# Cross attention with a ternary feed-forward on one core: high and low keys of four heads stacked on 64 rows

## The reference, cut to what matters

```
q = layernorm(x) @ Wq + bq          # 32 x 56 x 128, split in 16 heads of 8
k = ctx @ Wk + bk                   # 32 x 1500 x 128
v = ctx @ Wv + bv
scores = einsum('bhqd,bhkd->bhqk', q, k) / sqrt(8)
scores = where(mask == 0, -1e9, scores)
out = softmax(scores) @ v           # heads joined again, 32 x 56 x 128
x = x + out @ Wo + bo
x = x + bitlinear(gelu(bitlinear(layernorm(x), w1)), w2)
```

## Time and profile before

| | us |
|---|---|
| median of 3 runs | 959.67 |
| lowest and highest run | 958.06, 964.99 |
| profiled execution | 959.75 |
| its span | 958.0 |
| TensorE busy | 887.8 (93%) |
| VectorE busy | 753.1 (79%) |
| ScalarE busy | 673.4 (70%) |
| GpSimd busy | 231.5 (24%) |

### The profile page before, as it was taken

How to read it: one execution, slowest core, us unless ns; L and a number is a source line. 1 busy time by engine, 2 the same in 40 slices (tenths; PEclk the granted TensorE clock), 3 DMA queues, 4 the chain that set the end, 5 groups by cost and what they waited for, 6 DMA issues and landing times.

```text
span 958.0 us, 33628 instructions
## 1 busy us (share of the span) xinstructions
PE 887.8 (93%) x11716; PEld 694.2 (72%) x11716; DVE 753.1 (79%) x2593; ACT 673.4 (70%) x1272; POOL 231.5 (24%) x253
## 2 busy tenths in 40 slices
PE   3767989999999999999999999999999999999983
PEld 2344767777787787778787777777787777778772
DVE  3687568888788878888788888888787888888744
ACT  2543667777887877777886777777887777777661
POOL 6310142230222222130222222131222222031200
PEclk9788999999999999999999999999999999999997
DMA  5520221122222211122222211122222111220000
GB/s 130 127 62 1 63 61 29 42 57 60 63 60 63 59 34 47 46 60 60 63 60 63 53 32 50 51 60 60 63 60 61 49 32 50 56 60 0 4 2 6
DMA packets 59375, 49.34 MB, mean 52 GB/s; under 512 B 2785, under 2 KB 55633, under 8 KB 59345
## 3 DMA queue, kind: packets, MB, share of 16 engines
q1 hardware_dynamic: 57551, 48.11, 19.0%
q10 hardware_dynamic: 1793, 0.83, 0.4%
HBM read 47.91 MB, written 0.92 MB: 51 GB/s over the span
## 4 chain that ended last, share of the span: by engine, by line
issue 66%; POOL 18%; PE 7%; DVE 5%; ACT 1%; DMA 1%; POOLq 1%; DVEq 0%; ACTq 0%
POOL k_lo L573 8%; POOL qry_hi L565 4%; POOL qry_lo L566 4%; PE ps_p L820 2%; DMA ctx_sb<-in_ctx_dram 1%; PE ps_p L803 1%; DVE max_junk L1091 1%; POOL q_lo L563 1%; POOL q_hi L562 1%; PE ps_v L856 1%; PE ps_p L744 1%; ACT probs L659 1%; POOL x_rows L581 0%; PE ps_p L741 0%; POOLq L556 0%
## 5 line engine op out<-in xcount | busy, mean ns | idle before, releaser
L1091 DVE CUSTOM_DVE_ANT_0 max_junk<-ps_p,mask_bias 120x500 bf16<-120x500 f32 x768 | 481.6, 675 | 125.3 <-PE ps_p L803 104.5
L659 ACT ACTIVATE probs<-ps_p 125x448 f32<-125x448 f32 x768 | 359.3, 551 | 87.0 <-PE ps_p L820 81.6
L573 POOL TENSOR_TENSOR k_lo<-k_full,k_hi 128x500 fp32r<-128x500 f32 x96 | 119.8, 1262 | 592.0 <-ACT k_hi L651 587.2
L856 PE MATMUL ps_v<-probs,vals 125*32 125x112 f32 x6144 | 162.9, 262 | 0.8 <-issue 0.4
L803 PE MATMUL ps_p<-k_hi,qry_hi 64*120 64x500 f32 x768 | 148.8, 413 | 15.6 <-POOL qry_hi L565 6.5
L820 PE MATMUL ps_p<-qry_hi,k_hi 64*125 64x448 f32 x768 | 158.6, 403 | 4.4 <-DVE seg_max L1091 1.7
L856 PEld LDWEIGHTS ps_v<-probs,vals 125*32 125x32 f32 x6144 | 146.9, 111 | 21.1 <-issue 17.7
L641 ACT ACTIVATE k_full<-ps_p,bk_sb 128x500 f32<-128x500 f32 x96 | 64.7, 674 | 123.1 <-PE ps_p L744 122.6
L820 PE MATMUL ps_p<-own_query,mask_bias 57*125 57x448 f32 x768 | 145.7, 368 | 0.0
L820 PE MATMUL ps_p<-qry_lo,k_hi 64*125 64x448 f32 x768 | 144.4, 366 | 0.0
L820 PE MATMUL ps_p<-qry_hi,k_lo 64*125 64x448 f32 x768 | 144.3, 365 | 0.0
(11 more groups left out here) (124 smaller groups left out, 831.5 us busy)
## 6 DMA issues: line engine op xcount, KB each, us to landing
ctx_sb<-in_ctx_dram SPq DMA_DIRECT2D x31, 750.0 KB
mask_sb<-in_mask_Bx1xSxS_ik_dram SPq DMA_DIRECT2D x64, 328.1 KB
own_query<-shift SPq DMA_DIRECT2D x64, 1.8 KB
out_dram<-x_rows SPq DMA_DIRECT2D x16, 56.0 KB, 1.6
ctx_sb<-in_ctx_dram ACTq DMA_DIRECT2D x1, 750.0 KB
x_rows<-in_x_dram SPq DMA_DIRECT2D x1, 672.0 KB, 10.9
w_sb<-in_L_ffn_w_dram SPq DMA_DIRECT2D x2, 256.0 KB, 8.8
x_rows<-in_x_dram SPq DMA_DIRECT2D x1, 224.0 KB, 5.9
```

The source lines that it names most:

```text
L573: pool.tensor_tensor(k_lo[:, p, at], k_full[:, (p + n) % 2, :], k_hi[:, p, at].bitcast(F32), ALU.subtract)\
L659: act.activation(probs[:, c % NP, h], ps_p[0:KC, BANK[how]["S", c, h], 0:HC], ACT.Exp)\
L856: mm = pe.matmul(ps_v[r:r + VT, col:col + PAIR], vals[:, p, c, t].rearrange("p a r -> p (a r)"), src, start=(c == 0 and t < 4), stop=(c == ...
L1091: dve.tensor_tensor_reduce(max_junk[0:MROWS, BANK[how][slot], :], ps_p[0:MROWS, BANK[how][slot], 0:SEG], mask_bias[0:MROWS, p, s * SEG:(s ...
```

## The change

The keys of a batch now lie in one array `keys` of two planes, 128 rows each. In plane 0 a half of 64 rows holds the high keys of its first four heads (32 rows) and their low keys (32 rows); in plane 1 it holds the low keys of the last four heads and their high keys. ScalarE writes the high part of all rows into both planes with one copy of 2 x 500 elements (`high_keys`). GpSimd makes the low part in a buffer of its own (`k_lo`, two segments deep), and SP moves it by DMA, 32 rows x 500 at a time, over the rows in `keys` that are to hold it (`place_low`, four DMAs a segment, three segments a batch). The queries are projected twice, so that the query of a head stands on both of its sets of rows (`wq_sb` with two planes of columns, `q_all`, `q_flag`, `q_hi`, `q_lo` twice as wide). `qry_lo` is masked with `head_of_high`, which has zeros on the rows of low keys.

A block of scores is now, for each four heads, one product of 64 rows with `qry_hi` (high and low keys at once) and one with `qry_lo`, each of 4 x 56 = 224 columns, and then the product with mask and shift of 448 columns. The maxima multiply the stacked rows too: as many matmuls of 500 columns as before, but they wait for the DMAs of the low keys. The probabilities get eight buffers instead of twelve.

```diff
+GH = HH // 2
+GR = GH * HD
-NP = NC
+NP = 2 * NG
...
-    "T0 T1 T2 X0 Q0 K0 K1 K2 F0",
+    "T0 T1 T2 X0 Q0 Q1 K0 K1 K2 F0",
...
+            def place_low(bt, n):
+
+                b, k, p = bt
+                made = NSEG * b + n + 1
+                at = slice(n * SEG, (n + 1) * SEG)
+                sp.wait_ge(k_lo_ready, made if isinstance(b, int) else sp.snap(made))
+                for h in range(2):
+                    for g in range(2):
+                        src, dst = SLOT * h + GR * g, SLOT * h + GR * (1 - g)
+                        sp.dma_start(keys[dst:dst + GR, p, g, at].bitcast(F32), k_lo[src:src + GR, (p + n) % 2, :].bitcast(F32))\
+                            .then_inc(k_lo_placed[p][n], 16)
...
-                put_q(pool.tensor_tensor(q_hi[:], q_flag[:], ones_f[:, 0:SQ], ALU.mult))
-                put_q(pool.tensor_tensor(q_lo[:], q_flag[:], q_hi[:].bitcast(F32), ALU.subtract))
+                put_q(pool.tensor_tensor(flat(q_hi[:]), flat(q_flag[:]), ones_f[:, 0:2 * SQ], ALU.mult))
+                put_q(pool.tensor_tensor(flat(q_lo[:]), flat(q_flag[:]), flat(q_hi[:].bitcast(F32)), ALU.subtract))
...
                 pool.wait_ge(k_hi_ready, NSEG * b + n + 1)
+                if n == 2:
+                    pool.wait_ge(k_lo_placed[p][0], 64 * (k + 1))
+                else:
+                    wait(pool, k_lo_placed[1 - p][n + 1], 64 * (k + p))
+                pool.tensor_tensor(k_lo[:, (p + n) % 2, :], k_full[:, (p + n) % 2, :],
+                                   keys[:, p, 0, at].bitcast(F32), ALU.subtract)\
...
-                act.activation(k_hi[:, p, at], k_full[:, (p + n) % 2, :], ACT.Copy).then_inc(k_hi_ready, 1)
+                act.activation(keys[:, p, :, at],
+                               k_full[:, (p + n) % 2, :].rearrange("p (g k) -> p g k", g=1).to_broadcast([D, 2, SEG]),
+                               ACT.Copy).then_inc(k_hi_ready, 1)
...
                 if r == 0:
-                    pe.wait_ge(k_hi_ready, NSEG * b + s + 1)
+                    pe.wait_ge(k_lo_placed[p][s], 64 * (k + 1))
...
-                products = [(hi, q_hi_of, HR), (lo, q_hi_of, HR), (hi, q_lo_of, HR),
-                            (bias, own_query[:, p, :, :], SQ + 1)]
-                for n in range(first, last):
-                    key, query, rows = products[n]
-                    for h in range(2):
-                        part = slice(SLOT * h, SLOT * h + rows)
-                        mm = pe.matmul(ps_p[0:KC, BANK[how]["S", c, h], 0:HC].rearrange("k (a q) -> k a q", a=HH),
-                                       key[part, :], query[part], start=(n == 0), stop=(n == 3))
+                for g in range(2):
+                    heads = slice(GH * g, GH * (g + 1))
+                    for part, query in enumerate((qry_hi[:, p, heads, 0:SQ], qry_lo[:, p, heads, :])):
+                        for h in range(2):
+                            rows = slice(SLOT * h, SLOT * (h + 1))
+                            pe.matmul(score_bank(c, h, how)[:, heads, :], keys[rows, p, g, at], query[rows],
+                                      start=(g == 0 and part == 0), stop=False,
+                                      skip_group_check=True)
```

More of the change, by code:

```diff
@@ L144 @@
 DVE_PASS = passes(
-    "Q0 some F0 bias0 bias1 bias2",
+    "Q0 Q1 some F0 bias0 bias1 bias2",
     " ".join(f"m{n}" for n in range(16)) + " some " + " ".join(f"m{n}" for n in range(16, 21))
@@ L262, in xattn_ffn @@
         some_diag = sb("some_diag", [128, SQ], BF16)
-        q_flag = sb("q_flag", [D, SQ])
-        q_hi = sb("q_hi", [D, SQ], F32R)
-        q_lo = sb("q_lo", [D, SQ], F32R)
+        q_flag = sb("q_flag", [D, 2, SQ])
+        q_hi = sb("q_hi", [D, 2, SQ], F32R)
+        q_lo = sb("q_lo", [D, 2, SQ], F32R)
         max_junk = sb("max_junk", [128, NBANK, SEG], BF16)
@@ L307, in xattn_ffn @@
         k_lo_ready = sem("k_lo_ready")
+        k_lo_placed = [[sem(f"k_lo_placed{p}_{n}") for n in range(NSEG)] for p in range(2)]
         vals_ready = sem("vals_ready")
@@ L474, in _ @@
             sp.dma_start(w2_sb[:], w2).then_inc(ff_loaded, 16)
+            for n in range(NSEG):
+                place_low(batch(0, 0), n)
             sp.dma_start(wo_sb[:], wo).then_inc(wo_loaded, 16)
@@ L484, in _ @@
                     sp.dma_start(wo_rows[VT * g:VT * g + VH, t, :], wo[at:at + VH, :]).then_inc(wo_rows_loaded, 16)
+            for n in range(NSEG):
+                place_low(batch(0, 1), n)
             place_shift(batch(0, 0))
@@ L757, in fill @@
                 elif kind == "Q":
-                    mm = pe.matmul(bank[:, 0:4 * PAIR], wq_sb[:], xnt[:, n % 2, :], start=True, stop=True)
+                    mm = pe.matmul(bank[:, 0:4 * PAIR], wq_sb[:, n % 2], xnt[:, n // 2 % 2, :], start=True, stop=True)
                 elif kind == "Z":
```

120 lines of the change are left out of this document (81 added, 39 removed).

## The result

| | before | changed |
|---|---|---|
| median of 4 runs, us | 959.49 | 998.32 |
| lowest and highest run | 958.06, 964.99 | 992.09, 1001.43 |
| span of the profiled execution | 958.0 | 996.6 |
| loop on TensorE, us a turn (pair of batches) | 54.16 | 56.46 |
| first turn ends at | 186.0 | 194.2 |

The ratio is 1.039, with a 95% interval of 1.033 to 1.045: slower, where 934 us had been forecast. A turn is the distance of two taken branches of TensorE's loop, as a mean over 13. The 38.6 us of the spans are 8.2 at the start, 13 x 2.30 = 29.9 in the loop, and 0.5 at the end.

The account below looks back on a forecast made before the run. TensorE was taken to set the pace most of the time, VectorE and ScalarE close behind. Per pair -1.1 - 1.4 + 0.6 = -1.9 us, over 15 pairs -28.5, plus 3 at the start: 959.75 to 934 us, range 905 to 961.

Parts of the forecast that it names:

- TensorE sets the pace most of the time: Whole loop: TensorE mostly limits the 54.2 us pair, VectorE and ScalarE close behind; only savings where TensorE limits count.
- TensorE is the limit: Even step, first to last maximum: TensorE saves 2.1 us, of which 1.4 us a pair was taken, bounds 0.6 and 2.1.
- the end would still gain 0.9 us: End of the odd step: last values products start 0.9 us after the last exponential; part of the 1.1 us gain.
- The handover: From odd to even step: longer copy and wider query operations add 0.6 us a pair, bounds 0.4 and 1.6.
- ScalarE's longer copy: Copy of the high keys, 1000 elements instead of 500: +0.42 us three times a batch, 0.3 put on the handover's chain.
- The lower bound, the copy hidden: Handover from odd to even step: at least 0.4 us a pair if ScalarE's longer copy is hidden.
- The DMAs: Low keys, twelve a batch: 0.35 to 0.68 us an issue, landing 1.6 later; covered except 0 to 1 us at segment 1.
- Rival B: Low keys come late for maxima of segments 0 and 1, even step; with 2.5 us more, 972 us; chance 0.10.
- The start: Before the loop: low keys' DMAs and the shift queue behind other transfers, costing 3 us, bounds 0 and 6.
- The narrow pair: Scores on TensorE: a pair of 224 columns takes 0.11 us, bounds 0.10 and 0.185; a block saves 0.175 us.
- rival D: Scores on TensorE: narrow pairs are not cheap, break-even 0.154 us a pair; 1008 or 1307 us; chance 0.06.
- the rule on weight loads: Skill's rule: loads overlap matmuls only across row groups; a narrow pair would cost 0.10 + 0.10 us, a block 1.0.

Follow-up runs that it names:

- e2: The changed kernel with 60 one-column matmuls (120 instructions) ahead of TensorE's other work: 972.91 us, ratio 1.012 to the kernel before.
- e8: As e2 with the narrow products alone: no low keys moved, high keys copied once, low keys' share of scores left out: 948.74 us, ratio 0.988.
- e6: As e2, with the low keys of segment 1 made ahead of `qry_lo` on GpSimd: 959.77 us, ratio 1.000.
- e5: As e2, with SP's queue reordered at the start, low keys and shift of batch 0 moved ahead: 973.99 us, ratio 1.014.
- e10: As e8, with half of the narrow products, those of the low queries, left out: 936.66 us, ratio 0.975 to the kernel before.

## Why the prediction was wrong

**The step that failed first** is one that is missing. The sum went through engines, queues and DMAs, and had no term for TensorE's instruction stream: it put it at nothing without a reason. The loop went from 1605 to 1701 instructions, came to lie over one more stretch of fetching, and stood still 2.6 us at each taken branch. 998.3 less e2's 972.9 is 25.4 us of the 38.8. No rival held it either. Without the stall the kernel is still slower than before and outside the range of 905 to 961, so the terms below failed too. The page's row for q8, 18 packets in 958 us, was there to be asked: why does this loop need none, and when would it?

**"TensorE sets the pace most of the time"** and, of the even step, "TensorE is the limit" are the second failure, a mis-sized term. In e8 the even step gave 0.84 us (forecast 1.4, bounds 0.6 and 2.1), the odd one 0.36 (forecast 1.1, lower bound 0.9), and half of the products left out on top of that gave 0.73 us for 5.0. In the odd step ScalarE's row of exponentials was read rightly as full, and the claim that the end would still gain 0.9 us was wrong: the values products stand behind two maxima in TensorE's order, and in both traces VectorE's last maximum releases those (at 447.81 before, 446.57 in e8). The values products begin 0.5 us later, 0.7 us ahead of the last exponential's end in both kernels.

**The handover** came out near its sum, partly by luck. Of the +0.6, 0.3 were for the wider operations on VectorE and GpSimd, and from `q_flag` to the first maximum the runs show 0.30. The other 0.3 were for ScalarE's longer copy, and they did not come: e6 copies 1000 elements and e8 500, and their last stretches are 23.28 and 23.24 us. In their place stand 0.24 in the quantisation, whose cause was not foreseen (below). The lower bound, the copy hidden, is 0.3 by the text's own terms, not 0.4. `q_hi` takes 0.42 us, the copy of the high keys 1.04, both as worked out.

**The DMAs** had the right place and the wrong sum. The text put "0 to 1 us" on segment 1, and e6 shows 0.84 a turn. An issue took 0.61 us (0.35 to 0.68 forecast), a landing 2.0 instead of 1.6. The Trainium skill (DMA: Bandwidth & Descriptors, "Anatomy of one DMA") gives 2.0 us as the fixed cost, for DMAs issued by GpSimd; these, issued by SP, took as long. Rival B named the mechanism and asked for 2.5 us a turn. That its 972 us are e2's 972.9 is luck: in e2 a turn came to +0.26 instead of -1.9, and the start to 8.

**The start** cost 8 us, above its bound of 6. e8 has 2 of them without transfers of low keys and with the short copy, so some 6 belong to these two; e5 shows that the queue's order alone is not the cure. Which wait it is stays open.

**The narrow pair** at 0.11 us was right, and rival D and the rule on weight loads are refuted here: pairs on the same 64 rows start 0.11 us apart, though one record of a load lasts 0.19. One premise of rival D was wrong: the trace of before does hold single-pass matmuls under 448 columns, the 6144 values products of 112 columns, one record for each call.

## What to carry to other kernels

Ahead of any change to a long loop on TensorE, count its instructions and look at the fetch packets inside it in the profile: a stall marked "issue" right behind the branch, once a turn, is the sign, and a few dummy instructions ahead of the loop can be worth 25 us, or cost 108. A comparison of two kernels with long loops is only fair when both are placed well. Where the fullest engine stands at 90% and the next two at 80% and the order is written out, cost a saving by taking the work away altogether in one experiment: in e10 1 us of TensorE's work bought 0.15 us.
